# Cross attention of a decoder layer: probabilities made directly with keys on partitions, instead of transposed there

## What is computed

```python
q = (Q @ Wq + bq).reshape(b, -1, H, HD).transpose(0, 2, 1, 3)      # H = 16, HD = 8
k = (K @ Wk + bk).reshape(b, -1, H, HD).transpose(0, 2, 1, 3)      # 512 keys
scores = jnp.einsum('bhqd,bhkd->bhqk', q, k) / scale               # 256 queries
scores = jnp.where(mask == 0, -jnp.inf, scores)
attn = jax.nn.softmax(scores, axis=-1)
ctx = jnp.einsum('bhqk,bhkd->bhqd', attn, v)
```

## Time and profile before

| | |
|---|---|
| times of three runs | 217.65, 218.81, 218.91 us (median 218.81) |
| span of the profiled execution | 219.2 us |
| PE busy | 202.3 us (92%) |
| DVE / ACT / POOL busy | 163.7 / 126.4 / 90.6 us |

### The profile page before, as it was taken

How to read it: one execution, slowest core, us unless ns; L and a number is a source line. 1 busy time by engine, 2 the same in 40 slices (tenths; PEclk the granted TensorE clock), 3 DMA queues, 4 the chain that set the end, 5 groups by cost and what they waited for, 6 DMA issues and landing times.

```text
span 219.2 us, 4318 instructions
## 1 busy us (share of the span) xinstructions
PE 202.3 (92%) x1536; PEld 147.0 (67%) x1536; DVE 163.7 (75%) x424; ACT 126.4 (58%) x297; POOL 90.6 (41%) x136
## 2 busy tenths in 40 slices
PE   7599999799999799699796999999898999999993
PEld 7346466576767467456463665666565899999993
DVE  2628657878687799567999999998995685548843
ACT  2325436767575485536694989989696532372220
POOL 1989703764747466400899930000120002711332
PEclk9979999999999999979999999999999999999999
DMA  5960735999552003300601500000000000000000
GB/s 156 376 176 0 191 48 67 138 111 137 82 151 94 0 0 89 59 0 14 204 1 36 111 0 0 3 1 3 1 0 3 0 3 1 3 0 24 3 0 24
DMA packets 11740, 12.67 MB, mean 58 GB/s; under 512 B 848, under 2 KB 10064, under 8 KB 11648
## 3 DMA queue, kind: packets, MB, share of 16 engines
q1 hardware_dynamic: 11480, 12.20, 25.8%
q0 software_dynamic: 96, 0.20, 0.4%
q10 hardware_dynamic: 144, 0.01, 0.1%
HBM read 10.96 MB, written 1.44 MB: 57 GB/s over the span
## 4 chain that ended last, share of the span: by engine, by line
PE 74%; DVE 14%; issue 4%; ACT 3%; POOL 2%; DMA 2%; POOLq 0%; DVEq 0%
PE ps L830 12%; PE ps L792 8%; PE ps L721 7%; PE ps L736 7%; PE ps L851 7%; PE ps L629 7%; PE ps L708 6%; PE ps L770 6%; PE ps L752 5%; PE ps L641 4%; DVE q_t L1040 3%; DVE x_hat L915 2%; DMA x_in<-in_x 2%; PE ps L808 1%; DVE prob_t L1113 1%
## 5 line engine op out<-in xcount | busy, mean ns | idle before, releaser
L446 POOL TENSOR_TENSOR prob<-prob,rec 128x512 f32<-128x512 f32 x32 | 32.6, 1041 | 29.6 <-DVE rec L1095 29.6
L1040 DVE CUSTOM_DVE_ANT_0 q_t<-ps,mask_add 128x512 f32<-128x512 f32 x64 | 41.3, 682 | 2.1 <-PE ps L752 2.1
L531 ACT ACTIVATE prob<-ps,low 128x256 f32<-128x256 f32 x64 | 29.5, 475 | 18.4 <-DVE low L1030 18.4
L556 ACT ACTIVATE q_t<-q_t,low 128x512 f32<-128x512 f32 x44 | 29.4, 719 | 10.4 <-DVE low L1040 10.4
L386 POOL TENSOR_SCALAR var_eps<-mean_var 128x2 f32<-128x2 f32 (+1 forms) x5 | 1.1, 226 | 68.3 <-DVE mean_var L907 68.3
L792 PE MATMUL ps<-ident,q_t 128*128 128x128 f32 x176 | 23.4, 275 | 3.9 <-DVE place_o L1113 2.0
L792 PEld LDWEIGHTS ps<-ident,q_t 128*128 128x128 f32 x176 | 19.9, 141 | 9.2 <-issue 4.5
L1030 DVE TENSOR_REDUCE low<-ps 128x2 f32<-128x512 f32 x32 | 20.5, 683 | 6.3 <-PE ps L708 6.2
L1110 DVE COPY prob_t<-ps 128x512 f32<-128x512 f32 x32 | 20.6, 683 | 2.8 <-PE ps L736 2.8
L541 ACT ACTIVATE q_t<-ps 128x512 f32<-128x512 f32 x18 | 10.6, 598 | 21.0 <-PE ps L830 21.0
L752 PE MATMUL ps<-k_stack,q_stack 72*128 72x512 bf16 x64 | 19.3, 386 | 1.6 <-issue 1.6
(11 more groups left out here) (167 smaller groups left out, 422.3 us busy)
## 6 DMA issues: line engine op xcount, KB each, us to landing
k_stack<-k_dram SPq DMA_DIRECT2D x9, 256.0 KB
q_stack<-q_dram SPq DMA_DIRECT2D x6, 192.0 KB
wg<-in_L_ffn_w_gate SPq DMA_DIRECT2D x1, 1024.0 KB, 20.3
wu<-in_L_ffn_w_up SPq DMA_DIRECT2D x1, 1024.0 KB, 27.9
k_dram<-prob SPq DMA_DIRECT2D x1, 768.0 KB, 3.6
prob_t<-in_ctx SPq DMA_DIRECT2D x2, 256.0 KB, 4.0
w_in<-in_L_attn_Wq SPq DMA_DIRECT2D x1, 512.0 KB, 6.3
w_in<-in_L_attn_Wk SPq DMA_DIRECT2D x1, 512.0 KB, 7.1
```

The source lines that it names most:

```text
L446: nc.gpsimd.tensor_tensor(pr, pr, rec1[:, s % 2, r, :].unsqueeze(2).to_broadcast([P, C, S]), ALU.mult).then_inc(s_norm1, 1)
L531: e = nc.scalar.activation(prob1[:, s % 3, r, c * S:(c + 1) * S], ps[:, 2 * (s % 2) + r, c * S:(c + 1) * S], ACT.Exp, bias=low1[:, s % 2, ...
L556: nc.scalar.activation(prob2[n % 3][:, c, :], score2[n % 2][:, c, :], ACT.Exp, bias=low2[:, n % 2, c:c + 1], scale=-1.0).then_inc(s_exp2, 1)
L1040: nc.vector.tensor_tensor_reduce(out=score2[n % 2][:, c, :], in0=ps[:, 2 * (n % 2) + c, :], in1=mask_add[:, c, :], scale=1.0, scalar=3e38, ...
```

## The change

The probabilities no longer pass through a transpose. For the cross attention the kernel now does this:

- **Keys and queries in two float32r parts** (high and remainder) instead of three bfloat16 parts: three products of parts (Q_ROWS, K_ROWS) make 24 rows, plus 2 rows for the shift, so 26 of a block of 32 rows per head. Four heads of a group lie in the four row blocks. The stacks are made by 12 DMAs each, from SBUF to SBUF, with no DRAM between.
- **Scores twice.** scores2 (new L814) as before, queries on partitions, now only to find the maximum: top_scores2 on VectorE adds the mask and writes back into the same PSUM bank. shift_rows puts the negated maxima of four heads in the two extra rows of the queries (three products into PSUM, a ScalarE copy to q2_shift). scores2_t then computes the scores again with keys on partitions and the maximum already subtracted: per half (256 keys) of a pair of heads two products of the identity with the transposed mask (L851, bfloat16, 512 columns), then four products of 26 rows (L856, 256 columns).
- **Exponential straight to its place.** exp2 reads PSUM and writes prob2_t, 128 x 512 at a time. turn2 and both copies of its results are gone.
- **Order.** The cross attention goes by pairs j of heads, with the scores of pair j + 3 (LEAD) beside the transposed scores of pair j. Both kinds have a ring of three PSUM banks.
- **GpSimd.** The bias DMAs are issued before the memsets; k2_stack, q2_stack and shift_cols are filled by memsets; the first 8 expert weight splits are moved into steps g = 8 to 15 of the self attention.

```diff
-k2_parts = prob1_flat[:, 0:PARTS * TK // 2].bitcast(BF16)...
+k2_parts = prob1_flat[:, 0:2 * TK].bitcast(F32R).rearrange("p (j t) -> p j t", j=2)
@@ SP
-load(k2_dram.rearrange("j r t -> r j t"), k2_parts, d_kdram)
-sp.wait_ge(d_kdram, 16)
-for j in range(PARTS):
-    for i in range(PARTS):
...
+def stack(dst, parts, rows, s):
+    for i in range(HG):
+        for j, part in enumerate(rows):
+            r = ROW_TILE * i + SHIFT_ROWS + j * HD2
+            src = parts[ROW_TILE * i:ROW_TILE * (i + 1), part, :]
+            load(dst[r:r + HD2].bitcast(F32), src.bitcast(F32), s)
@@ GpSimd
-if 0 <= n - SPLIT_N < 2 * (NE + 1):
-    split_weights(n - SPLIT_N)
+if 0 <= g - SPLIT_G < 2 * (NE + 1):        # SPLIT_G = 8, SPLITS_EARLY = 8
+    split_weights(g - SPLIT_G)
@@ ScalarE
-act.wait_ge(d_kdram, 16)
+act.wait_ge(d_kstack, 16 * HG * len(K_ROWS))
-nc.scalar.activation(prob2[n % 3][:, c, :], score2[n % 2][:, c, :], ACT.Exp,
-                     bias=low2[:, n % 2, c:c + 1], scale=-1.0).then_inc(s_exp2, 1)
+nc.scalar.activation(prob2_t[n % PT_SLOTS][:, 2 * half:2 * half + 2, :],
+                     ps[:, E_BANK + v % RING, :].rearrange("p (k t) -> p k t", k=2), ACT.Exp,
+                     scale=SCALE2).then_inc(s_exp2, 1)
@@ TensorE
+def shift_rows(gr):
...
+    mm(bank[:, 0:S], ident_r[:, :], q2_stack[:, hg, b * S:(b + 1) * S], start=True, stop=False)
+    for c in range(C):
+        last = mm(bank[:, c * P:(c + 1) * P], shift_cols[:, gr % 2, c, :], ident_r[:, :],
+                  start=False, stop=c == C - 1)
+def scores2_t(j, half):
...
+    exp_bank_free(EXP_UNIT[2 * j + 1, half])
+    for bank in banks:
+        mm(ps[:, bank, :], ident_b[:, :], mask_t_add[...], start=True, stop=False)
+    for k2 in range(2):
+        for r, bank in enumerate(banks):
+            last = mm(ps[:, bank, k2 * S:(k2 + 1) * S], k2_stack[rows_of(h), h // HG, t:t + P],
+                      q2_shift[rows_of(h), gr % 3, :], start=False, stop=k2 == 1)
-def turn2(n):
...
@@ VectorE
-nc.vector.tensor_tensor_reduce(out=score2[n % 2][:, c, :], in0=ps[:, 2 * (n % 2) + c, :],
+nc.vector.tensor_tensor_reduce(out=bank, in0=bank,
-nc.vector.tensor_copy(prob2_t[(n - LAG_T) % PT_SLOTS][:, 0:2, :],
-                      ps[:, PT_BANK, :].rearrange("p (k t) -> p k t", k=2)).then_inc(s_pt2a, 1)
```

More of the change, by code:

```diff
@@ L1125, in _ @@
                         ).then_inc(s_o2, 1)
+                for what in BETWEEN.get((g, 1), ()):
+                    between(what)
+                if 0 <= j < N_PAIRS - LEAD:
+                    top_scores2(j + LEAD, 1)
                 if FFN_G <= g < FFN_G + FFN_EARLY:
```

477 lines of the change are left out of this document (286 added, 191 removed).

## The result

The changed kernel takes 243.95 us (median of four runs, 243.41 to 248.0), the kernel before 218.77: a ratio of 1.113, 95% interval 1.105 to 1.120. The forecast of 214 was wrong by 30 us, and on the wrong side. The profiled execution has a span of 241.9 us where 213.6 had been worked out.

The account below looks back on a forecast made before the run. Three engines were nearly even in the steady cross attention, with the chain on TensorE. 219.2 - 5.9 (cross attention) + 2.5 (tail) - 2.2 (prologue) = 213.6 profiled, 213.2 as median, given as 214; range 205 to 225.

Parts of the forecast that it names:

- with the DMA issues first all four take about 1.3: Prologue: four normalising operations on VectorE end at 8.3 instead of 10.5 us, a gain of 2.2.
- They lie under the projections: Prologue: GpSimd's 5.8 us of further fills are hidden if the value parts come before about 27 us.
- ScalarE's wait: Self attention: ScalarE waiting for the key stack before its first exponential was listed as a sign of error, without size.
- The first transposed scores at 101.3: Cross attention's start: maxima begin at 92.1, shift at 99.7, then 1.6 us more to the first transposed scores.
- TensorE's work per group, 7.9: Steady cross attention: masks, both scores, values, outputs, shift and 1.2 us of shape changes sum to 7.9 us.
- Waits per group, 0.3: Steady cross attention: waits and extra pieces stay at 0.3 us per group, making 8.2 in all.
- Rival 4: Cross attention: engines wait in turn, TensorE for a maximum; 0.8 us more per group gives 220; chance 0.12.
- The opening groups: Cross attention's start: the opening group has 6.0 us on TensorE but 7.5 of VectorE work, adding 1.5.
- Early splits, cost 0: Self attention: expert weight splits hide in GpSimd's idle time, expert loads landing early enough; cost 0.
- rival 3: Self attention: GpSimd waits for the expert loads until near 69; +6 us, perhaps 2 for the clock, 221; chance 0.08.
- Tail, +2.5: After the first expert product: 1.0 us of group 6's values plus about 1.5 waiting for its outputs' copy.
- Rivals 1 and 2: Cross attention: row blocks serial (226) or changes at 0.2 (223), chance 0.20; TensorE loses less, 203, chance 0.12.

Follow-up runs that it names:

- keys apart: Changed kernel with the keys' two parts stored outside the probabilities' storage, so ScalarE need not wait for the key stack; profiled span 234.7 us.
- mended kernels: Changed kernel with GpSimd's fills waiting for the normalisation, the keys' parts stored outside the probabilities, or both; profiled spans 230.4 to 244.8 us.
- seven traces: Profiled executions of the changed kernel and its four prologue-fixed variants; first to last transposed scores took 65 us plus 0.40 per us at half clock.
- swap: Changed kernel with both prologue fixes, second query stack on two queues, every second pair's last two row products behind its transposed scores; median 222.5 us.
- 18 filling products: Unused TensorE products in the cross attention's opening; with prologue fixes and two queues ratio 1.016 to the kernel before, with later reorderings too 1.011.

## Why the prediction was wrong, point by point

- **Prologue, "with the DMA issues first all four take about 1.3".** This step failed, and it is the largest term: 13.4 us later instead of 2.2 earlier. I read in the earlier trace rows that the fill held the normalisation, and then took the recorded starts at their word: issues to 8.7, normalisation done by 8.3. The added fills make an unbroken row of 8.2 us, and that row held operations that had started ahead of it: the four took 10.97. With the fills behind them they took 1.12, and with the keys apart as well the self attention ended 2.4 earlier than before.
- **"They lie under the projections"**, of the 5.8 us of further fills: wrong for the same reason. What they hold is VectorE, ahead of the projections.
- **The key stack.** The prediction gave no price to ScalarE's wait; it only named it as a sign of being wrong. It cost 4.7 alone. The step left out was to follow the twelve issues and who stands behind them: 0.75 us each where nine had taken 0.35, all in one queue, and 11.1 us more until the last had landed.
- **The first transposed scores at 101.3.** Right in its own terms: 14.3 us after the last minimum were worked out, 14.8 came (115.2 after 100.4), and the same 14.8 in the mended kernels.
- **TensorE's work per group, 7.9.** Right: 7.8 in the chain. Its pieces hold their changes of shape: masks 2.05, transposed scores 1.5, scores for the maximum 1.3, values 2.15, shift 0.5, turned outputs 0.4. Their parts in the forecast were 1.76, 1.4, 0.96, 2.14, 0.24 and 0.22, with 1.2 of changes by themselves. The closing split of that sum is off (0.6 net of small products, where 1.4 + 0.96 + 0.24 - 1.76 is 0.84); nothing hangs on it. Two products of a pair start together:

```profile
115.50 0.39 PE L856 MATMUL ps<-q_shift,k_stack 26*128 26x256 f32 x2
...
115.72 0.28 PE L856 MATMUL ps<-q_shift,k_stack 26*128 26x256 f32 x2
```

- **Waits per group, 0.3.** Mis-sized: 0.8, and five to eight times. Rival 4 had the mechanism word for word (a product needs the maximum three units earlier) but was priced as a separate case and not as a share of the forecast. It is worth about 3 us over the stage.
- **The maximum's write to PSUM** cost nothing next to the earlier trace rows: two of them start 0.61 us apart.

```profile
160.32 0.69 DVE L1149 CUSTOM_DVE_ANT_0 ps<-ps,mask_add 128x512 f32<-128x512 f32 x1
...
160.93 0.73 DVE L1149 CUSTOM_DVE_ANT_0 ps<-ps,mask_add 128x512 f32<-128x512 f32 x1
```

- **The clock.** No term stood for it in the sum, though the earlier trace rows show it falling behind one pause of 1.65 us. The opening has more pauses than before. From the first to the last transposed scores the stage takes 74.0 us in the changed kernel with 23.9 at the half level; by the line through the seven traces it would be 65 with none. So the price in the profiled execution is about 9 us (an estimate), and this is the largest part of the 12.2 of this stage. What is left of them is covered by the 0.5 of the start and the 3 or so of the waits.
- **The opening groups.** My sum had about 14 us for the first two. The traces have 20.5 with 16.4 at the half level (changed kernel), 19.7 with 13.7 (keys apart) and 18.1 with 10.2 (swap): less 0.40 for each us at that level, 13.9, 14.2 and 14.0 (estimates). So they came as counted. The 19.5 with the clock held (100.34 to 119.82) hold the 18 filling products.
- **Early splits, cost 0.** Right, but in part by luck; rival 3 fell. The two large expert loads were issued at 50.5 and 50.9, not before 40, close to the 51 from which the wait was to cost something. They landed 5.4 and 7.9 us later, and the division ahead of the first split ended at 73.9, not at 60.5, so the split follows it at once:

```profile
71.84 2.04 POOL L477 TENSOR_TENSOR prob<-prob,rec 128x512 f32<-128x512 f32 x2 [1.56 <-DVE rec L1216]
73.82 0.40 POOL L433 CAST w_in_parts<-wg 128x256 fp32r<-128x256 f32 x1
```

- **Tail, +2.5.** 3.0 measured; the copy of the outputs does stand behind the table load and the first activation (191.16, 192.46, then 192.95).
- **Rivals 1 and 2** fell: row blocks overlap, and the masks cost what was counted. The rival that was missing is that a change of the order in the prologue has its own stalls, at another price than the stage at which the change aims.

## What to carry to other kernels

When a change moves or adds work of an engine that holds another one, take its whole unbroken row as the length of the stall, and put the held work ahead by a semaphore instead of by arithmetic on recorded starts. Price what a change adds outside its aim (fills, stacking transfers, and each engine that waits for them) as carefully as its core: here TensorE's work in the core was right within 0.1 us per group, and the rest was worth over 20 us. And where TensorE's margin is small, a pause at a stage's start is dearer than its length, since the clock may stay down long behind it; but work added only to keep the clock up cost as much here as it brought.

## What the hardware showed that I had not expected

- A row of GpSimd fills held VectorE's copies from SBUF to SBUF for all of its length, from before its recorded start (8.65) to its end: 10.4 us for an operation of 0.3. With a semaphore between the fills, two operations came through at each join.
- TensorE's clock stayed at 1.2 GHz for 44 us in one stretch with the engine busy over 95% of it, and the same kernel in another execution had a mean clock of 0.954, which makes some 21 us at that level in all (an estimate): 226.8 to 243.8 us for one program. Each us at the half level cost the stage 0.40 us.
- A DMA from SBUF to SBUF that gathers 32 partitions into 8 took SyncE 0.75 us to issue (12 in 9.04), against 0.35 for one from DRAM (9 in 3.14).
- Leaving out the masks, 2.5 of TensorE's 7.8 us per group, gave 223.7 to 224.0 us in three executions of four, at mean clocks of 0.838 to 0.877, and 210.0 in the fourth, at 0.942.
